# Attention: the product of probabilities and values from high and low parts, three single-pass products for one in full fp32

## What is computed

```python
q, k, v = x @ w_q, x @ w_k, x @ w_v            # x: layer norm of the block's input
scores = einsum('bqd,bkd->bqk', q, k) / sqrt(256)
scores = where(causal, scores, -inf)
a = softmax(scores, axis=-1)
y = einsum('bqt,btd->bqd', a, v)               # this product is changed
```

## Time and profile before

| | us |
|---|---|
| median of 3 runs | 3001.99 |
| lowest, highest | 2996.59, 3004.52 |
| the profiled execution, its own time | 3004.03 |
| its span in the profile | 3002.2 |
| attention: first join matmul of row 0, of row 15 | 2122.11, 2462.19 |

### The profile page before, as it was taken

One profiled execution on the slowest core, in us unless ns is written; L12 is line 12 of the kernel. 1 busy time (PEld: TensorE's weight loads), 2 busy tenths in 40 slices (PEclk: granted clock), 3 DMA queues, 4 the chain that ended last, 5 costly groups with the idle time before them and its releaser, 6 DMA issues. The chain is left out here.

```text
span 3002.2 us, 48292 instructions
## 1 busy us (share of the span) xinstructions
PE 2777.6 (93%) x16944; PEld 2232.6 (74%) x16944; DVE 2243.1 (75%) x3482; ACT 1754.1 (58%) x3175; POOL 2216.2 (74%) x1565
## 2 busy tenths in 40 slices
PE   7899999999999999999976999999898986999998
PEld 3566666666566666666666999999777776999998
DVE  4999999989999999989886565656465554656564
ACT  5776777667766777677754454444445443545443
POOL 4889999999999999999996676664254446666664
PEclk9999999999999999999988999999999997999999
DMA  6222321132212321122122455553222223555552
GB/s 175 97 89 73 102 91 56 63 96 94 71 54 87 102 88 44 59 87 77 57 66 95 111 135 119 126 121 74 58 83 74 70 88 109 124 123 125 120 122 36
DMA packets 184204, 273.19 MB, mean 91 GB/s; under 512 B 35687, under 2 KB 156174, under 8 KB 175816
## 3 DMA queue, kind: packets, MB, share of 16 engines
q1 hardware_dynamic: 148680, 227.92, 24.1%
q0 software_dynamic: 35328, 42.76, 8.0%
HBM read 188.89 MB, written 94.72 MB: 94 GB/s over the span
## 5 line engine op out<-in xcount | busy, mean ns | idle before, releaser
L570 POOL TENSOR_TENSOR dbu<-du,bb 128x1024 f32<-128x1024 f32 x512 | 1195.8, 2362 | 21.9 <-DVE hs L730 16.6
L730 DVE TENSOR_TENSOR_SCAN hs<-da,dbu 128x1024 f32<-128x1024 f32 x512 | 1152.6, 2279 | 76.2 <-ACT da L665 34.5
L665 ACT ACTIVATE da<-delta 128x512 f32<-128x512 f32 x1024 | 568.1, 594 | 228.2 <-DVE hs L730 225.4
L835 PEld LDWEIGHTS yT<-ident,hs 128*128 128x128 f32 x4096 | 486.9, 146 | 138.0 <-issue 97.1
L835 PE MATMUL yT<-ident,hs 128*128 128x128 f32 x4096 | 543.8, 283 | 10.4 <-DVE hs L730 10.4
L1464 POOL TENSOR_TENSOR ffn_w_lo<-ffn_w,ffn_w_hi 128x512 fp32r<-128x512 f32 x240 | 319.9, 1350 | 78.0 <-ACT ffn_w_hi L1459 76.2
L1550 PE MATMUL ffn_hbank<-ffn_w_hi,ffn_hT_hi 128*128 128x256 f32 x1280 | 366.9, 287 | 1.6 <-DVE ffn_hT_lo L1537 1.6
L1552 PE MATMUL ffn_hbank<-ffn_w_hi,ffn_hT_lo 128*128 128x256 f32 x1280 | 361.2, 282 | 0.0
L1551 PE MATMUL ffn_hbank<-ffn_w_lo,ffn_hT_hi 128*128 128x256 f32 x1280 | 360.5, 282 | 0.0
L1515 PE MATMUL ffn_hbank<-ffn_rowsT_hi,ffn_w_hi 128*128 128x320 f32 x1024 | 318.6, 311 | 4.0 <-POOL ffn_w_lo L1464 3.3
L1516 PE MATMUL ffn_hbank<-ffn_rowsT_lo,ffn_w_hi 128*128 128x320 f32 x1024 | 318.1, 311 | 0.0
(11 more groups left out here) (279 smaller groups left out, 4966.4 us busy)
## 6 DMA issues: line engine op xcount, KB each, us to landing
bb<-b_rows SPq DMA_DIRECT2D x64, 1024.0 KB, 4.7
ffn_w<-L_ffn_W SPq DMA_DIRECT2D x60, 1024.0 KB, 8.8
slots<-empty SPq DMA_DIRECT2D x40, 530.0 KB, 7.4
empty<-slots SPq DMA_DIRECT2D x16, 662.5 KB, 5.0
ffn_rows<-slots SPq DMA_DIRECT2D x16, 662.5 KB, 4.9
xt<-L_attn_a_x SPq DMA_DIRECT2D x16, 512.0 KB
a_xn<-L_attn_a_x SPq DMA_DIRECT2D x16, 512.0 KB, 3.8
x_after_mamba<-a_xn SPq DMA_DIRECT2D x16, 512.0 KB
```

Of the source, the lines that this page charges most:

```text
L570: pool.tensor_tensor(dbu[:, s % DEEP], du[:, dt, :].unsqueeze(1).to_broadcast([P, SN, T]), bb[:, q * SN:(q + 1) * SN, :], ALU.mult).then_i ...
L665: ins = act.activation(da[:, s % 2, i, :], delta[:, par, dt, :], ACT.Exp, scale=-float(q * SN + i + 1))
L730: dve.tensor_tensor_scan(flat[0], flat[1], flat[2], 0.0, ALU.mult, ALU.add).then_inc(scanned.sem, 1)
L835: mm = pe.matmul(yT[:, j * P:(j + 1) * P], hs[:, s % DEEP, i, j * P:(j + 1) * P], k.ident[:], start=False, stop=(q == QS - 1 and i == SN - ...
```

## The change

The copies of P0 to P3 and of V0 and V1 by ScalarE write fp32r tensors, the high parts. VectorE subtracts them from the same banks for the low parts (`probs_low`, `values_low`), so it is now VectorE that frees these six banks. Each product in `mix_values` becomes three single-pass ones: high by high, high by low, low by high. TensorE's order of jobs and ScalarE's order stay.

```diff
--- before.py
+++ after.py
@@ -1781,9 +1781,9 @@
 A_RING = (("T0", 1), ("P1", 2), ("O0", 2), ("RT1", 3), ("T1", 1), ("P2", 2), ("O1", 2), ("P3", 2), ("O2", 2),
           ("O3", 2), ("RL", 3), ("G0", 1), ("G1", 1), ("V0", 1), (None, 0), ("V1", 1), ("RP", 3), (None, 0),
           ("S0", 1), ("S1", 1), ("S2", 1), ("RT0", 2), ("P0", 1), ("S3", 1))
-A_ACT = (("S2", 2), ("P1", 2), ("S3", 2), ("P2", 2), ("RT1", 3), ("P3", 2), ("V0", 1), ("V1", 1), ("S0", 1),
-         ("S1", 1), ("P0", 1), ("RT0", 2))
-A_DVE = (("T0", 1), ("O0", 2), ("O1", 2), ("T1", 1), ("O2", 2), ("O3", 2), ("RL", 3), ("G0", 1), ("G1", 1), ("RP", 3))
+A_ACT = (("S2", 2), ("S3", 2), ("RT1", 3), ("S0", 1), ("S1", 1), ("RT0", 2))
+A_DVE = (("T0", 1), ("P1", 2), ("O0", 2), ("T1", 1), ("P2", 2), ("O1", 2), ("P3", 2), ("O2", 2), ("O3", 2), ("RL", 3),
+         ("G0", 1), ("G1", 1), ("V0", 1), ("V1", 1), ("RP", 3), ("P0", 1))
 A_LAST, KEPT = 4, 4
 
 class Flow:
@@ -1841,9 +1841,10 @@
         x_kept, x3 = sb("x_kept", [P, KEPT - 2, NT, C]), sb("x3", [P, 2, NT, C])
         xn, xnT_hi, xnT_lo = k.att_xn, sb("xnT_hi", [P, 2, NC, T], F32R), sb("xnT_lo", [P, 2, NC, T], F32R)
         gT_hi, gT_lo = (sb(n, [P, 2, NC, T], F32R) for n in ("gT_hi", "gT_lo"))
-        v = sb("v", [P, 2, NT, C])
+        v_hi, v_lo = (sb(n, [P, 2, NT, C], F32R) for n in ("v_hi", "v_lo"))
+        p_split, v_split = Count(sem("p_split"), NT), Count(sem("v_split"), 2)
         top, bias = sb("top", [P, 2, NT]), sb("bias", [P, 2, NT])
-        pr, prT = sb("pr", [P, NT, T]), sb("prT", [P, NT, T])
+        pr, prT_hi, prT_lo = sb("pr", [P, NT, T]), sb("prT_hi", [P, NT, T], F32R), sb("prT_lo", [P, NT, T], F32R)
         total, inverse = sb("total", [P, 2, NT]), sb("inverse", [P, 2, NT])
         ring = ctx.enter_context(nc.psum_tensor("a_ring", [P, BANKS, T], F32))
 
@@ -1908,6 +1909,17 @@
         def turned_low(dve, row, par, c):
             dve.wait_ge(t_hi.sem, t_hi.at(row, c + 1))
             dve.tensor_tensor(xnT_lo[:, par, c, :], bank_of(f"T{c}"), xnT_hi[:, par, c, :].bitcast(F32),
+                              ALU.subtract).then_inc(dve_took.sem, 1)
+
+        def probs_low(dve, row, i):
+            dve.wait_ge(p_split.sem, p_split.at(row, i + 1))
+            dve.tensor_tensor(prT_lo[:, i, 0:(i + 1) * P], bank_of(f"P{i}")[:, 0:(i + 1) * P],
+                              prT_hi[:, i, 0:(i + 1) * P].bitcast(F32), ALU.subtract).then_inc(dve_took.sem, 1)
+
+        def values_low(dve, row, par, h):
+            dve.wait_ge(v_split.sem, v_split.at(row, h + 1))
+            dve.tensor_tensor(v_lo[:, par, 2 * h:2 * h + 2, :].rearrange("p j c -> p (j c)"), bank_of(f"V{h}"),
+                              v_hi[:, par, 2 * h:2 * h + 2, :].rearrange("p j c -> p (j c)").bitcast(F32),
                               ALU.subtract).then_inc(dve_took.sem, 1)
 
         def joined_low(dve, row, par, m):
@@ -1986,8 +1998,8 @@
             wait_product(act, row, f"V{h}")
             if h == 0:
                 wait_product(act, row - 2, "O3")
-            act.activation(v[:, par, 2 * h:2 * h + 2, :].rearrange("p j c -> p (j c)"), bank_of(f"V{h}"),
-                           ACT.Copy).then_inc(act_took.sem, 1)
+            act.activation(v_hi[:, par, 2 * h:2 * h + 2, :].rearrange("p j c -> p (j c)"), bank_of(f"V{h}"),
+                           ACT.Copy).then_inc(v_split.sem, 1)
 
         def probs(act, row, par, i):
 
@@ -2000,7 +2012,7 @@
         def probs_turned(act, row, i):
             wait_product(act, row, f"P{i}")
             wait_product(act, row - 1, f"O{i}")
-            act.activation(prT[:, i, 0:(i + 1) * P], bank_of(f"P{i}")[:, 0:(i + 1) * P], ACT.Copy).then_inc(act_took.sem, 1)
+            act.activation(prT_hi[:, i, 0:(i + 1) * P], bank_of(f"P{i}")[:, 0:(i + 1) * P], ACT.Copy).then_inc(p_split.sem, 1)
 
         def route_turned(act, row, c):
             wait_product(act, row, f"RT{c}")
@@ -2062,7 +2074,10 @@
             wait_taken(pe, row, f"P{i}")
             wait_taken(pe, row, "V1")
             for j in range(i + 1):
-                mm = pe.matmul(bank[:, 0:C], prT[:, i, j * P:(j + 1) * P], v[:, par, j, :], start=(j == 0), stop=(j == i))
+                ks = slice(j * P, (j + 1) * P)
+                pe.matmul(bank[:, 0:C], prT_hi[:, i, ks], v_hi[:, par, j, :], start=(j == 0), stop=False)
+                pe.matmul(bank[:, 0:C], prT_hi[:, i, ks], v_lo[:, par, j, :], start=False, stop=False)
+                mm = pe.matmul(bank[:, 0:C], prT_lo[:, i, ks], v_hi[:, par, j, :], start=False, stop=(j == i))
             mm.then_inc(ring_mm.sem, 1)
 
         def route_turn(pe, row, par, c):
@@ -2185,11 +2200,14 @@
                     if runs(turn - 1):
                         turned_low(dve, turn - 1, 1 - par, 0)
                     if runs(turn - 2):
+                        probs_low(dve, turn - 2, 1)
                         add_attention(dve, turn - 2, par, 0)
-                        add_attention(dve, turn - 2, par, 1)
                     if runs(turn - 1):
                         turned_low(dve, turn - 1, 1 - par, 1)
                     if runs(turn - 2):
+                        probs_low(dve, turn - 2, 2)
+                        add_attention(dve, turn - 2, par, 1)
+                        probs_low(dve, turn - 2, 3)
                         add_attention(dve, turn - 2, par, 2)
                         add_attention(dve, turn - 2, par, 3)
                         route_stats(dve, turn - 2, par)
@@ -2201,13 +2219,16 @@
                     if runs(turn) and not is_first(turn):
                         take_stats(dve, turn, par)
                     if runs(turn - 1):
+                        values_low(dve, turn - 1, 1 - par, 0)
                         row_max(dve, turn - 1, 1 - par, 0)
+                        values_low(dve, turn - 1, 1 - par, 1)
                         row_max(dve, turn - 1, 1 - par, 1)
                     if runs(turn - 3):
                         route_place(dve, turn - 3, 1 - par)
                     if runs(turn - 1):
                         row_max(dve, turn - 1, 1 - par, 2)
                         row_max(dve, turn - 1, 1 - par, 3)
+                        probs_low(dve, turn - 1, 0)
 
                 turns(dve, one_turn)
```

## The result

The changed kernel takes 3049.74 us (median of 4 runs, 3045.86 to 3051.54), 1.0148 times the time before, 95% interval 1.0119 to 1.0177: slower by 1.5%. The prediction was 3070 with a range of 3012 to 3105: the direction and the chain of waits hold; the lateness that it added on top hardly came, and the time is 20 us lower. A second comparison gave 1.0169, 1.0143 to 1.0195.

The account below looks back on a forecast made before the run. TensorE was taken to bound the attention turn (19.5 us of issuing). 23.3 + 1.5 lateness + 2.2 clock = 27.0 us against 22.67; over 15 turns 65 us, plus 3 for the last row: +68, 3070 us, range 3012 to 3105.

Parts of the forecast that it names:

- the lateness: ScalarE copies P3 late after its transposes end on TensorE; taken as 1.5 us a turn, added in full ahead of O2.
- The hand chain: Walk through one attention turn from T0: TensorE's waits for low parts in VectorE's queue, less the saving, add 3.6 us.
- The subtractions: Six more on VectorE a turn, 0.28 to 0.69 us each, 3.3 us together; VectorE does not become the bound.
- The saving of TensorE: Mixing products: three single-pass at 0.354 us replace one full at 0.436; 0.82 us a turn, 13 us in all.
- The turn without lateness: Attention turn with P3 copied on time and the clock held: 19.5 + 3.6 + 0.2 = 23.3 us.
- The clock: TensorE's clock falls behind a 4.1 us gap ahead of O2 in 8 turns of 10: 0.8 x 2.7 = 2.2 us.
- rival A: Lateness of P3's copy belongs to full-fp32 products and goes with them; clock holds, turn 23.3, 3014 us; chance 0.17.
- signs of being wrong: O1 and O2 start without a wait, or ScalarE copies P3 at once and turns last 23, or joins under 22 apart.
- signs of being right: TensorE waits 0.8, 1.0, 3 us or more ahead of O0, O1, O2; clock under 1.00 mostly; joins 25 to 29 apart.
- B: Rival: low parts reach TensorE in time, only its saving counts; 2989 us, as low as 2940 without lateness; chance 0.06.
- The rule named there: Improving a kernel generally means improving its most-contended engine; taking work from TensorE would then make it faster.
- C: Rival: P3's lateness grows to 3.5 us, clock falls every turn; turn 29.5 us, time 3107; chance 0.15.

Follow-up runs that it names:

- e6_after_no_sends: Changed kernel without POOL's indirect sends in the attention for rows 0 to 14: 3037.17 us (one run).
- e4_no_v_low: Changed kernel without the values' low parts (two subtractions of 512 columns a row fewer; second product takes the high part): 3052.86 us, ratio 1.0229 to the kernel before.
- e5_before_no_sends: Kernel before the change without POOL's indirect sends in the attention for rows 0 to 14: 2941.87 us (one run).
- e7_reorder_no_sends: Changed kernel with VectorE's queue reordered as in e1_reorder and without the attention's indirect sends of rows 0 to 14: 2936.94 us (one run).
- e3_full_waits: Changed kernel with one full fp32 product in place of three; low parts still made and waited for, but not multiplied: 3026.82 us, ratio 1.0145 to the kernel before.
- e2_no_low: Changed kernel without any low parts or their six subtractions; three single-pass products stay, all high by high: 3008.95 us, ratio 1.0074 to the kernel before.
- e1_reorder: Changed kernel, same work, VectorE's low parts of P0 to P3 moved earlier in its queue: 3008.97 us, ratio 1.0081 to the kernel before.
- e8_reorder_again: The program of e1_reorder, sends included, run on another chip: 2955.16 us, ratio 1.0032 to a kernel before of 2945.86.

## Why the prediction was right, and where it was off

**The hand chain** held. Starts behind T0 in us, as forecast and in the turn shown above:

| | forecast | measured |
|---|---|---|
| O0 | 1.4 | 2.21 |
| O1 | 3.9 | 4.42 |
| P3 | 4.6 | 5.20 |
| O2 | 7.64 | 8.21 |
| O3 | 8.84 | 9.40 |
| RL | 10.26 | 10.86 |

The gap between P3's issue and O2 is 2.57 as forecast (2478.25 - 2475.24 - 0.44). Everything lies some 0.6 later, and that enters with the first step, "P0's low part is queued behind the row maximum of S3, whose bias ends at 1.08". It ends at 1.91 (2471.95 - 2470.04). ScalarE's exponent of S3 waits for that bias, and T0's copy stands behind it, so T0's low part and with it P1's are 0.5 later as well. The duration was right and the queue was read too short: e6_after_no_sends has O0 at 1.38, as forecast. I had written of the low parts of V that nothing on TensorE needs them for 7 us, and charged T0 with 0.2. What they do is hold VectorE's queue for V1's copy, and that copy waits on ScalarE behind a norm that waits for a send. e4_no_v_low takes away the low parts, e6_after_no_sends the sends, and in both the idle time ahead of O0 comes down to 0.56. O0's loss was so 1.53 in place of 0.75, O1's 0.57 in place of 0.95, since part of its wait had been waited already.

**The subtractions** cost what the rows gave: 0.28, 0.42, 0.55 and 0.69 us in the timeline above.

**The saving of TensorE** was mis-sized, 0.82 a turn where 0.44 was there (e5_before_no_sends against e7_reorder_no_sends). I had taken 0.118 from the evenly spaced products inside V0 for all thirty, and the first of a job takes 0.20; these four make 0.33 of the 0.38 that was missing.

**The turn without lateness** was forecast as 23.3. It is 23.71 in the last turn, and 23.95 on average in e3_full_waits, less the 0.44. Two errors partly cancel in it, which is luck: the base of 19.5 was too high (19.15 without sends, since the idle time of 0.81 that I took off understates what lateness cost that turn; O2 and O3 took 4.15 us in it, and 3.03 in e5_before_no_sends), and the hand chain was 0.6 too short.

**The lateness**, 1.5 a turn, is the term that was mis-sized most: it is 0.25 on average. "Lateness of P3 now adds in full" holds: in the five turns with 0.55 to 0.96 of it the gap ahead of O2 grows by as much, from 2.57 to 3.1 to 3.5. With 0.25 in place of 1.5 and all else kept, the forecast would have been 19 us lower, 3051. What failed is the step that carried the lateness of the kernel before over unchanged. The kernels of one chip show half a pattern, P3's lateness on average: 2.48 in e2_no_low, where no mixing product waits long for a low part, 1.08 in e1_reorder with short pauses, 0.04 in e3_full_waits with long ones, but 0.75 in e4_no_v_low with pauses nearly as long. So pauses of TensorE go with less lateness and do not settle it; the cause stays open.

**The clock** was about right in size, by luck, and wrong in its condition. Forecast was 2.2 us a turn; 25.58 - 23.71 = 1.9 is what all turns have above the last, and TensorE's busy time is as much above that turn's (21.47 on average against 19.53). But I had let the clock fall because the gap ahead of O2 would be 4.1 us, with the lateness, and rival A has it hold behind 2.57. By that rule the small lateness would have taken the falls away too, for a turn of 23.55 and 15 x 0.88 + 3 = +16, which is 3018. The clock fell all the same, in 13 turns in place of 12, and a turn with a fall cost 2.2 us more on average (15 x 1.9 / 13), not 2.7. I had laid the falls to the length of the gap alone, and e3_full_waits has the gap of 2.41 with a clock of 1.00 in 13 turns of 15, where the changed kernel has it under 1.00 in 13 of 15 (gap 2.41 to 3.34) and e6_after_no_sends in all 15 (2.41). Behind this gap it is the single-pass products that bring the falls; how, no run shows.

**The rivals.** A's mechanism is refuted by e2_no_low. Its statement that the lateness goes came true in 10 turns of 15 all the same, by another way, and its time of 3014 did not, since the clock did not hold. So one of the signs of being wrong, that ScalarE copies P3 at once, appeared in most turns; the signs of being right came only in part: the wait ahead of O2 is 2.41 to 3.34 where 3 or more was said, and the joins lie 23.7 to 27.1 us apart, where it was 25 to 29. B needed the low parts in time. Its order exists, e7_reorder_no_sends, and gives 19.10 in place of the 18.7 that I had worked out. The rule named there (the Trainium skill, Perfetto Trace Analysis, Identifying Performance Opportunities) pointed to a gain; TensorE was the busiest engine by its share of the span (93%), work was taken from it, and the kernel lost 1.5%; in the better order, without sends, a turn gained 0.05 us. C did not come: the lateness shrank, and the slowest turn is 27.1, not 29.5.

**What I could not have read**: that the kernel before loses about 53 us to lateness in these turns (340.1 - 287.2), and that this goes with the sends and not with the mixing products. I had put the sends' times beside it and named no mechanism. It sets the ratio: +95 us without sends, +50 with them on the same chip.

## What to carry to other kernels

When a second engine gets a step between a copy and the product that needs it, write its queue in the order in which the consumer asks, and ask of every job behind a new one what it now waits for: six subtractions of together 3.3 us lengthened the stretch from T0 to the router by 4.2 us in the one order, and cost a wait of 0.4 in the other. Price a split product with the first product of each group, not with those in the middle of a long run. And before a small effect is read off a profile, see what else pauses the bound engine: here transfers of another engine masked about half of the cost on one chip, and on two others the kernel before hardly felt them, by its time (2945.5 and 2945.9 us, 2941.9 without).

## What the runs showed of the hardware

With POOL's indirect sends in the attention a signal of TensorE can reach its reader late, up to 3.80 us behind the recorded end (e2_no_low); without them it was 0.04 in every turn of the three kernels that were run so. In the kernel before, the 15 turns take 340.1 us with the sends and 287.2 without. The sends are not enough for it: the same program with the sends at the same place had 1.28 us of it on one chip and 0.04 on another. In e3_full_waits, with pauses of some 1.2 and 2.4 us in each turn, it was not there at all.

Behind the same gap of 2.41 us ahead of O2, TensorE's granted clock stayed at 1.00 in 13 of 15 turns with full fp32 products (e3_full_waits), and was under 1.00 in all 15 with three single-pass products, on the same chip (e4_no_v_low, its gap 2.41 or more) and on another (e6_after_no_sends, 0.81 to 0.93). In e1_reorder, e7_reorder_no_sends and e8_reorder_again, where no gap ahead of a mixing product is over 1.12 us, the single-pass products keep 1.00 in all turns but the first. Over the seven products of O2 and O3 a three-pass product of 128x128 by 128x256 took 0.380 us, a full fp32 one 0.433.
